# A rounded feed-forward phase in a gated cross-attention stack: row scales and bias without diagonals, another order of rounding, products and bank reads

## The reference, cut to what matters

```python
def quant_act_uint8(x):
    s = jnp.maximum(jnp.max(x), EPS) / 255.0            # one scale for the whole tensor
    return jnp.clip(jnp.round(x / s), 0.0, 255.0) * s, s
def quant_weight_int8_perchannel(w):
    s = jnp.maximum(jnp.max(jnp.abs(w), axis=1, keepdims=True), EPS) / 127.0
    return jnp.clip(jnp.round(w / s), -128.0, 127.0) * s, s[:, 0]
def quant_linear(x, w, b):
    xq, s_in = quant_act_uint8(x)
    wq, s_w = quant_weight_int8_perchannel(w)
    bq = jnp.round(b / (s_in * s_w)) * (s_in * s_w)
    return jnp.einsum('btd,fd->btf', xq, wq) + bq
h = relu(quant_linear(x, w1, b1))     # w1 (1024, 256)
return quant_linear(h, w2, b2)        # w2 (256, 1024)
```

## Time and profile before

| | us |
|---|---|
| median of 3 runs | 1348.64 (1346.47 to 1349.34) |
| the profiled execution, its own time | 1337.3 |
| its span from the first to the last instruction | 1335.3 |
| PE busy | 1205.5 (90%) |
| DVE busy | 687.5 (51%) |
| ACT busy | 470.8 (35%) |
| POOL busy | 290.7 (22%) |
| phase 3, from its first transposes to `phase_over` | 468.8 to 548.0 |

### The profile page before, as it was taken

How to read it: one execution, slowest core, us unless ns; L and a number is a source line. 1 busy time by engine, 2 the same in 40 slices (tenths; PEclk the granted TensorE clock), 3 DMA queues, 4 the chain that set the end, 5 groups by cost and what they waited for, 6 DMA issues and landing times.

```text
span 1335.3 us, 19939 instructions
## 1 busy us (share of the span) xinstructions
PE 1205.5 (90%) x7169; PEld 763.1 (57%) x7171; DVE 687.5 (51%) x1989; ACT 470.8 (35%) x903; POOL 290.7 (22%) x370
## 2 busy tenths in 40 slices
PE   4999979999999964799999799994799999999996
PEld 2544544334667822555556499994445456666663
DVE  5566445468555586676666522223645874222224
ACT  1055434443222174125444133331465531222220
POOL 4200011011200003121013522222431343222220
PEclk9699999999999986879989599998899999999998
DMA  9995020001000010000001866765000033444436
GB/s 242 267 274 172 1 57 3 0 1 63 1 1 1 1 36 0 2 20 2 1 17 52 280 201 214 214 202 180 15 1 1 33 113 121 150 154 150 157 112 201
DMA packets 107774, 124.09 MB, mean 93 GB/s; under 512 B 16834, under 2 KB 92222, under 8 KB 107678
## 3 DMA queue, kind: packets, MB, share of 16 engines
q1 hardware_dynamic: 100686, 103.93, 26.9%
q0 software_dynamic: 6992, 18.88, 3.8%
HBM read 73.93 MB, written 48.86 MB: 92 GB/s over the span
## 4 chain that ended last, share of the span: by engine, by line
PE 81%; DVE 7%; ACT 3%; issue 3%; POOL 3%; DMA 2%; SPq 1%; POOLq 0%; DVEq 0%; ACTq 0%
PE bank L1237 8%; PE bank L852 6%; PE bank L1271 5%; PE bank L778 5%; PE bank L1280 5%; PE bank L872 5%; PE bank L913 4%; PE bank L1063 3%; PE bank L916 3%; PE bank L1312 3%; PE bank L761 2%; PE bank L719 2%; PE bank L1020 2%; PE bank L925 2%; PE bank L955 2%
## 5 line engine op out<-in xcount | busy, mean ns | idle before, releaser
L1237 PE MATMUL bank<-scratch 128*128 128x320 f32 (+3 forms) x480 | 149.9, 468 | 0.0
L2114 DVE TENSOR_REDUCE scratch<-bank 128x2 f32<-128x308 f32 x256 | 103.8, 470 | 58.9 <-PE bank L852 58.5
L1391 ACT ACTIVATE scratch<-bank 128x512 f32<-128x512 f32 x192 | 99.1, 602 | 64.9 <-PE bank L879 48.1
L1237 PEld LDWEIGHTS bank<-scratch 128*128 128x128 f32 (+1 forms) x480 | 85.3, 181 | 55.1 <-issue 22.8
L1759 POOL TENSOR_SCALAR rstd<-mv 128x4 f32<-128x4 f32 x36 | 9.2, 254 | 474.3 <-DVE mv L1895 460.7
L2628 DVE TENSOR_TENSOR scratch<-scratch,bank 128x320 f32<-128x320 f32 (+3 forms) x60 | 31.4, 525 | 152.5 <-PE bank L1237 152.3
L852 PE MATMUL bank<-scratch 32*128 32x308 f32 x512 | 81.2, 516 | 3.8 <-DVE scratch L2114 1.7
L2611 DVE TENSOR_TENSOR scratch<-bank,weights 128x512 f32<-128x512 f32 x39 | 27.0, 692 | 103.1 <-PE bank L1271 103.1
L1271 PEld LDWEIGHTS bank<-scratch 128*128 128x128 f32 x624 | 77.4, 195 | 2.7 <-issue 0.8
L1271 PE MATMUL bank<-scratch 128*128 128x128 f32 x624 | 77.8, 279 | 0.4 <-ACT scratch L1581 0.4
L872 PE MATMUL bank<-scratch 32*128 32x512 f32 x384 | 74.3, 626 | 1.0 <-ACT scratch L1453 0.7
(11 more groups left out here) (392 smaller groups left out, 2244.2 us busy)
## 6 DMA issues: line engine op xcount, KB each, us to landing
scratch<-in_L_ffn_W SPq DMA_DIRECT2D x47, 512.0 KB, 4.0
x_slots<-zeros SPq DMA_DIRECT2D x1, 17680.0 KB, 78.5
scratch<-y_back SPq DMA_DIRECT2D x16, 512.0 KB, 8.0
scratch<-in_L_ffn_w_gate SPq DMA_DIRECT2D x16, 352.0 KB, 3.1
scratch<-in_L_ffn_w_up SPq DMA_DIRECT2D x16, 352.0 KB, 4.0
x_slots<-zeros SPq DMA_DIRECT2D x1, 5200.0 KB, 95.4
scratch<-x_slots SPq DMA_DIRECT2D x39, 130.0 KB, 3.0
y_back<-zeros SPq DMA_DIRECT2D x1, 4352.0 KB, 38.4
```

The source lines that it names most:

```text
L1237: last = pe.matmul(bk[0:fn, 0:n], w[s][:, k, m * P:m * P + fn], moving(k), start=k == 0, stop=k == DK - 1)
L1391: act.activation(v["PT"][:, n % 2, j, :], bk[:], ACT.Exp, scale=float(v["hd"]) ** -0.5).then_inc(RP.read, 1)
L2114: dve.tensor_reduce(v["mx"][:, TPC * c + t, r, 2 * m:2 * m + 2], bk[:, 0:2 * M].rearrange("p (e k) -> p e k", k=M), AX.X, ALU.max)\
```

## The change

Nothing else in the program changes. In step 2 the transposes of chunk c + 1 stand in the middle of the products of chunk c, on PE and on ACT. In step 4 the diagonal of the weights' own scales `sw2` is made by POOL in phase 2, multiplied by `ones` in phase 3 before the first maxima, and kept as a row on all partitions (`swR`). DVE makes from it, while the first product runs, `swT` (times the gate) and `bw` (the bias over the weights' scale). After `scale(1)` one multiplication gives the output scale `rowT`, and two operations on one partition give the rounded bias as a float32 row (`rb`). The three bias matmuls of a tile become one with a contraction of one partition. `b2` is loaded as a row on all partitions. In step 5 DVE reads the first bank between the roundings, and the statistics of phase 4's chunks 0 and 1 are taken among the last banks, with their inverse roots on POOL in phase 3.

```diff
 def quantised(p):                                   # PE
+    pe.wait_ge(diag_made, 1)
+    bk = RC.take(pe, p, "swR")
+    for d in range(DK):
+        last = pe.matmul(bk[:, d * P:(d + 1) * P], ones[:], v["diagS"][:, d, :], start=True, stop=True)
+    last.then_inc(RC.filled, 1)
     rows_of_maxima(0)
-    for n in range(NC + 1):
-        if n < NC: (transposes of chunk n)
-        if n:      (products of chunk n - 1)
+    turn(0)
+    for c in range(NC):
+        pe.wait_ge(RA.read, RA.n(p, "xT", c))
+        for f in range(FT1):
+            if f == FT1 // 2 and c + 1 < NC:
+                turn(c + 1)
+            (product of block f)
     rows_of_maxima(1)
-    pe.wait_ge(diag_made, 1)
-    bk = RC.take(pe, p, "rowT")
-    for d in range(DK):
-        last = pe.matmul(bk[:, d * P:(d + 1) * P], ones[:], v["diagT"][:, d, :], start=True, stop=True)
-    last.then_inc(RC.filled, 1)
 ...
-                for n in range(3):
-                    last = pe.matmul(bk[:, i * D:(i + 1) * D], onesb[:],
-                                     v["diagB"][:, n].rearrange("p d j -> p (d j)"), start=False, stop=n == 2)
+                if (c, q, i) == (0, 0, 0):
+                    pe.wait_ge(rows_made, 1)
+                last = pe.matmul(bk[:, i * D:(i + 1) * D], ones[0:1, :], v["rb"][0:1, :], start=False, stop=True)
 def quantised(p):                                   # ACT
+    bk = RC.get(act, p, "swR")
+    act.activation(v["swR"][:], bk[:, 0:D], ACT.Copy).then_inc(RC.read, 1)
+    (copy of turned chunk 0, then of chunk c + 1 in the middle of the relus of chunk c)
-        if c == 2:
-            bk = RC.get(act, p, "rowT")
-            act.activation(v["rowT"][:], bk[:, 0:D], ACT.Copy).then_inc(RC.read, 1)
 def attention16(p, L):                              # POOL
-        norm(p, range(0, 2))
+        if L == 0:
+            norm(p, range(0, 2))
         clear(p, L)
 def attention(p, L):                                # POOL, phase 2
-    norm(p + 1, range(0, 3))
+    norm(p + 1, range(0, 2))
+    q = ph[p + 1]
+    pool.wait_ge(wq_made, 2)
     for d in range(DK):
+        st.did(pool.tensor_scalar(q["diagS"][:, d, :], ident[:], q["sw2"][:, d:d + 1], None, ALU.mult))
     st.wait()
     pool.sem_inc(diag_made, 1)
+    norm(p + 1, [2])
-def scales_on_diagonals(p): (removed; in its place in phase 3:)
+    norm(p + 1, range(0, 2))
 def prepare(p, L, v):                               # DVE
-    if L in (0, 2):
+    if L == 0:
         x_norm(p, range(0, 2))
+    if L == 2:
+        for c in range(2):
+            normalise(p, c)
 def quantised(p):                                   # DVE
     for c in range(NC):
         if c == NC - 1:
+            maximum(*parts[0])
             normalise(p, c)
 ...
+    dve.wait_ge(RC.read, RC.n(p, "swR"))
+    st.did(dve.reciprocal(v["bw"][:], v["swR"][:]))
+    st.did(dve.tensor_scalar(v["swT"][:], v["swR"][:], tg[:, 5:6], None, ALU.mult))
+    st.wait()
+    st.did(dve.tensor_tensor(v["bw"][:], v["bw"][:], v["b2"][:], ALU.mult))
+    for n in range(1, len(parts)):
+        maximum(*parts[n])
     scale(1)
     dve.sem_inc(hs_ready, 1)
-    (rt, ri, rb: five operations on 128x2, then rows_made)
+    def rounded(c):
         if c == 0:
             st.did(dve.tensor_scalar(a, a, v["sc"][:, 7:8], ROUND, ALU.mult, ALU.add))
+            st.did(dve.tensor_scalar(v["rb"][0:1, :], v["bw"][0:1, :], v["sc"][0:1, 7:8], ROUND, ALU.mult, ALU.add))
             st.wait()
         else:
             dve.wait_ge(hs_made, c)
         dve.tensor_scalar(v["hi"][:, :, c * CH:(c + 1) * CH], a, ROUND, 255.0, ALU.subtract, ALU.min).then_inc(hi_made, 1)
+        if c == 0:
+            dve.tensor_scalar(v["rb"][0:1, :], v["rb"][0:1, :], ROUND, None, ALU.subtract).then_inc(rows_made, 1)
+            st.did(dve.tensor_scalar(v["rowT"][:], v["swT"][:], v["sc"][:, 5:6], None, ALU.mult))
-    (all four roundings, then the eight banks)
+    (rounded 0, 1, 2; bank 0; rounded 3; banks 1, 2, 3;)
+    for c in range(2):
+        for q in range(2):
+            down(2 + c, q)
+            if q == 0:
+                st.wait()
+                statistics(p + 1, c)
```

More of the change, by code:

```diff
@@ L475, in build @@
                 v["h"] = scratch.take((FT1, T))
[L477 to L478 removed]
+                v["diagT"] = scratch.take((DK, P))
+                v["swR"], v["swT"], v["bw"] = scratch.take((D,)), scratch.take((D,)), scratch.take((D,))
+                v["rowT"], v["rb"] = scratch.take((D,)), scratch.take((D,))
                 v["m"] = scratch.take((64,))
@@ new lines, in quantised, with turn @@
+                last.then_inc(RC.filled, 1)
+                rows_of_maxima(0)
+                def turn(c):
+                    pe.wait_ge(xi_made, c + 1)
+                    bk = RA.take(pe, p, "xT", c)
+                    o = bk[:].bitcast(BF16)
+                    for d in range(DK):
+                        for i in range(TPC):
+                            last = pe.transpose(o[:, d * CH + i * P:d * CH + (i + 1) * P],
+                                                v["xi"][:, TPC * c + i, d * P:(d + 1) * P], identb[:])
+                    last.then_inc(RA.filled, 1)
@@ new lines, in quantised @@
+                turn(0)
+                for c in range(NC):
+                    cs = slice(c * CH, (c + 1) * CH)
+                    pe.wait_ge(RA.read, RA.n(p, "xT", c))
+                    for f in range(FT1):
+                        if f == FT1 // 2 and c + 1 < NC:
+                            turn(c + 1)
+                        bk = RC.take(pe, p, "up", c, f)
+                        for k in range(DK):
+                            last = pe.matmul(bk[:], v["w1T"][:, k, f * P:(f + 1) * P], v["xT"][:, k, cs],
+                                             start=k == 0, stop=k == DK - 1)
+                        last.then_inc(RC.filled, 1)
@@ L1537, in quantised, with turned @@
                                    bk[:].bitcast(BF16).rearrange("p (f j) -> p f j", j=P), ACT.Copy).then_inc(RA.read, 1)
[L1538 to L1544, removed]
-                    for f in range(FT1 if n else 0):
-                        c = n - 1
+                bk = RC.get(act, p, "swR")
+                act.activation(v["swR"][:], bk[:, 0:D], ACT.Copy).then_inc(RC.read, 1)
+                def turned(c):
+                    bk = RA.get(act, p, "xT", c)
+                    act.activation(v["xT"][:, :, c * CH:(c + 1) * CH],
+                                   bk[:].bitcast(BF16).rearrange("p (d j) -> p d j", d=DK), ACT.Copy).then_inc(RA.read, 1)
+                turned(0)
+                act.wait_ge(hscale_made, 1)
+                for c in range(NC):
+                    for f in range(FT1):
+                        if f == FT1 // 2 and c + 1 < NC:
+                            turned(c + 1)
                         bk = RC.get(act, p, "up", c, f)
@@ L2322, in quantised, with maximum @@
                 scale(0)
+                parts = [(c, f, n) for c in range(NC)
+                         for f, n in (((0, 4), (4, 4)) if c < NC - 1 else ((0, 4), (4, 2), (6, 1), (7, 1)))]
+                def maximum(c, f, n):
+                    at = parts.index((c, f, n))
+                    dve.wait_ge(RC.read, RC.n(p, "up", c, f + n - 1))
+                    st.did(dve.tensor_reduce(v["m"][:, at:at + 1], v["h"][:, f:f + n, c * CH:(c + 1) * CH], AX.XY, ALU.max))
                 for c in range(NC):
```

83 lines of the change are left out of this document (20 added, 63 removed).

## The result

| | before | after |
|---|---|---|
| median, us | 1348.12 (1346.47 to 1349.34, 4 runs) | 1366.47 (1363.10 to 1367.84, 4 runs) |
| ratio, 95% interval | | 1.0133 (1.0121 to 1.0145) |
| profiled execution, its own time / span | 1337.3 / 1335.3 | 1363.1 / 1361.4 |

The change made the kernel 18.35 us slower. 1343.2 was forecast, in 1336.5 to 1348.5 (from the median of three runs of before, 1348.64; a fourth made it 1348.12). The measured time is that of the rival with a chance of 0.08, a clock that stays low during the second product (1366.5).

What follows compares the result with a forecast made beforehand. Phase 3 was taken as four stretches limited by ACT, PE's wait for POOL, PE, and DVE. Gains of 0.7, 10.6 and 2.1 less 8.0 lost made 5.4 us: 1348.64 to 1343.2, range 1336.5 to 1348.5.

Steps and rivals of the forecast that it cites:

- the rival with a chance of 0.08: PE's clock stays at 1.2 GHz during phase 3's second product, 1.6 us more a tile: 1366.5 us; chance 0.08.
- The head: Start of phase 3, bound by ACT: PE's first product starts earlier; 0.7 us gained, -1 to +1.
- The wait: PE's wait for POOL's diagonals before phase 3's second product goes; that product begins 10.6 us earlier.
- The second product: Phase 3's sixteen tiles on PE, 1.70 us each, 3.30 at the low clock: 29.5 us, 8.0 lost.
- The reason against it: Against the slow clock: the first product ran with PE stops for ACT and had 0.92 over its stretch.
- rows 7: Profile rows where two one-row products hold the loads 0.51 us after a 0.65 stop, in a low-clock stretch.
- the change of rows costs nothing: Rival for the second product: tile 1.30 us, 23.2 us in all, total 1336.9 us; chance 0.12.
- The join: From phase 3's last addition to PE's first transpose of phase 4: about 3.5 us, 2.1 gained, bounds 1.5 to 3.6.
- Phase 4 gives it back: Rival: head's reciprocal at 4.0 us, or longer low clock after 570, at most some 3 us: 1345 to 1348; chance 0.10.

Runs made afterwards that it cites:

- paired products: The changed kernel with the one-row float32 bias products of a bank's two tiles side by side, halving the row changes: 1346.78 us, one run.
- kept-busy run: The changed kernel with 16 and 26 idle matmuls around PE's transpose of the second maximum, tiles untouched: 1341.26 us, one run.
- set 4: Runs sharing one chip: before 1347.17 us, changed 1365.28, 128-row bias product 1341.86, that with later POOL memsets 1340.86, and with idle matmuls too 1339.53.
- version with later memsets: The changed kernel with 128-row bias product, idle matmuls, and POOL's phase 4 clearing held until both chunks are normalised: 1334.22 us, ratio 0.9911.
- all rows and kept busy: The changed kernel with the bias product over 128 rows and idle matmuls around the transpose of the second maximum: 1340.94 us, ratio 0.9956.
- head-only kernel: The kernel before with only the first product's transposes, and ACT's copies, moved among its products: 1338.75 us, one run.

## Why the prediction was wrong, step by step

- **The head, 0.7 gained: right.** 0.76, and 0.55 to 1.2 in the other kernels with this head. The reciprocal took 1.75 us, near the 1.6 from the slope of the rows and within the bounds of 0.35 and 4.0.
- **The wait, 10.6 gained: right.** 10.67. Nothing took POOL's place but the rounding on DVE.
- **The second product, 8.0 lost: this step failed**, in its sentence "I expect 4.8 us at 0.50 on its return, as before". It was 47.6 us at 0.50. The price of the row changes was taken slightly too high (1.70 and 3.30 a tile forecast, 1.60 and 2.97 measured); with it right and the clock as forecast the step would have cost (4.8/2.97 = 1.6 tiles, then 14.4 x 1.60 = 23.0, in all 27.8) 6.3 us, not 26.1. So the clock costs 26.1 - 6.3 = 19.8 us, more than the whole miss of this step (18.1).
  I took the low stretch as a time that PE must work off after an idle wait. The runs show that it depends on what PE works on. From the start of the second product it took the clock 3.9 to 5.3 us to rise with before's tiles (four profiles, behind 0.8 us of the scale product), 5.0 to 5.6 with 128 rows (four), 5.1 without the bias product, 5.4 with one bf16 row, 12.3 with paired products, 12.4 with 64 rows (one each), and in three profiles of the changed kernel it didn't rise in 47 us. One product's times spread by 1.4 us, so the first four can't be put in an order; the last three stand apart. In each of these PE shows as busy up to the rise.
- **The rival, right in time, half right in cause.** It held that small products and stops make a busy PE lose its clock, and argued from 570 to 583. The kept-busy run refutes that for these tiles. What happens is narrower: PE arrives at a clock of 0.50 (from 505.1 on), behind its waits for the second maximum and the rounding, and under these tiles it doesn't come back. And its figure came out partly by luck: the forecast plus 23.3 us had 1.6 us for each of 14.55 tiles and so a total product of 52.8 us, where it was 47.6, and the 4 us behind the join were not in it.
- **The reason against it was weak.** That the first product ran at 0.92 with stops said nothing of one-row products: its matmuls have 128 rows. The evidence there was, thin as it is, stood in rows 7: the trace's eight one-row products all lie where PE's columns take the low clock's time. (Four, at 58.2 to 60.7 us, at a granted clock of 0.50; for those of rows 7 the trace gives 1.00, but the two products of 256 float32 columns behind them take 0.98 us (23.17 to 24.15), and not twice 0.21.) I used them for a price and not for the clock.
- **The rival "the change of rows costs nothing"** (tile 1.30, 1336.9) describes the tile of the version with 128 rows well, 1.31: a single-row operand padded with zeros has no change to pay. That its first time is 1336.91 too is chance; it took 1341.86 in set 4.
- **The join, 2.1 gained: its size was off.** 1.5. I had the memsets slow the first `normalise` (2.9 us for four). But in the changed kernel they began beside the gated bias in front of it, which took 2.27 us, against 0.35 to 0.41 without them; the first four `normalise` then took their 1.6 us, the same as in the version with later memsets. With all rows and kept busy it was as I had it: 0.35 for the bias, and 3.2 us from the first `normalise` to PE's first transpose.
- **Phase 4 gives it back (0.10).** 4.0 us against "at most some 3". It is there, but the head-only kernel has it as well (4.3, one profile), so it doesn't need the slow second product.

Two things stay open. What PE must do for its clock to rise isn't settled: fewer stops, fewer float32 columns or more rows each came with a rise (the times above), and no one of these alone orders the kernels. And why the low stretch that begins 16 to 17 us into phase 4 lasts 13.6 us in the three profiles of before, and 20.5 with another 3.4 behind it in the changed and the head-only kernel, wasn't tried; nor why the same code begins phase 4 with 3 us at the low clock in one profile and 9 to 11 in another.

## What to carry to other kernels

Before you narrow a product to save streamed columns, look at the clock on which it starts: at a granted clock of 0.50 a tile that mixes full products with one-row float32 ones may not bring TensorE back (here not in 47 us), and 8 us of forecast loss become 26. If a one-row operand is to be added to a bank of 128-row products, pad it with zeros to 128 rows (here 2.97 us a tile became 1.31, and 1.3% slower became 0.45 to 0.65% faster). What a repair gains in one phase may not arrive in the time: compare the stretch behind it too, in more than one profile. A wait removed ahead of a product is not the product's only cost: check what the engine did just before it, and whether the new instruction mix is one that the trace shows rising from 0.50 to 1.00 (here the tiles with 128 rows did, after 5.0 to 5.6 us).

## What the runs showed of the hardware

- The granted clock of a PE that the profile calls busy (47.53 of 47.65 us) can stay at 0.50 as long as the tiles last, and the same instructions run at 1.00 from end to end when PE comes to them at 1.00 (25.69 busy us of 26.40). So what the profile counts as busy doesn't tell which of the two clocks it will be; what does is not shown.
- Two changes between 128 rows and one, in a stream of 128-row products, cost 0.41 us at a clock of 0.50 and 0.30 at 1.00 a tile. 64 rows cost the same as one (2.97 and 1.61 a tile); with 128 rows, 127 of them zeros, the tile took 1.31, where the columns alone make 1.30.
- A DVE multiplication of 128x256 beside POOL's memsets took 2.27 to 2.41 us, and 0.35 to 0.41 without them; eight `normalise` took 4.21 beside them and 2.66 without. Two of the memsets took 1.09 and 0.45 us beside the `normalise`, and 0.95 and 0.31 behind them. So each engine held up the other here; by what, no run shows.
- Before took 1336.2 us in one set and 1347.2 in another on the same chip. The changed kernel took 1354.25 us beside a run of before of 1336.3, and 1365.28 beside 1347.17: a ratio of 1.0134 both times (the first from one run each). So ratios within a set are compared here, and times of different sets only where it is said.
